# Slot stages in two phases, with half of the norm on GpSimd

## The reference

```
xn = layernorm(x)                              # 256 features
h = gelu([xn, slot_mean] @ w1.T + b1)          # 128
logits = (h @ w2.T + b2) / (|tau| + 0.1)       # 64 slots
topk_vals, topk_idx = top_k(logits, 8)
alpha = scatter(softmax(topk_vals), topk_idx)  # zero outside the 8
slot_input = einsum('bts,btd->bsd', alpha, xn) # over all tokens of a batch
gi = slot_input / (alpha.sum(tokens) + 1e-8)
S_new = GRU(gi, slots)
out = x + (alpha @ (S_new @ wv.T + bv)) @ wo.T + bo
```

## Time and profile before

| | us |
|---|---|
| median of 3 runs | 2550.9 (2548.64 to 2559.86) |
| the profiled execution: its own time | 2551.9 |
| its span, first to last instruction | 2550.1 |
| first slots stage in it | 1819.4 to 1986.2 (the next part's first instruction) |
| second slots stage in it | 2432.3 to 2550.1 |

### The profile page before, as it was taken

How to read it: one execution, slowest core, us unless ns; L and a number is a source line. 1 busy time by engine, 2 the same in 40 slices (tenths; PEclk the granted TensorE clock), 3 DMA queues, 4 the chain that set the end, 5 groups by cost and what they waited for, 6 DMA issues and landing times. The chain is left out here.

```text
span 2550.1 us, 40275 instructions
## 1 busy us (share of the span) xinstructions
PE 2180.0 (85%) x14544; PEld 1305.5 (51%) x14544; DVE 1894.2 (74%) x2586; ACT 1819.4 (71%) x3103; POOL 1615.2 (63%) x1407
## 2 busy tenths in 40 slices
PE   0798898988989989899898998987367699999967
PEld 0345454554545545455454554544234377887744
DVE  4389888898888988889888898888474455555543
ACT  0598889988899888998989989897162244444452
POOL 1089898898988989889898898989310411222010
PEclk9999999999999999999999999999668799999979
DMA  5404224043241532414314143140400211111031
GB/s 188 104 14 117 74 52 117 27 107 77 49 117 35 136 81 53 117 41 93 91 35 117 43 92 92 34 108 17 169 19 29 96 30 34 29 29 29 22 114 66
DMA packets 129930, 184.25 MB, mean 72 GB/s; under 512 B 13634, under 2 KB 76098, under 8 KB 129348
## 3 DMA queue, kind: packets, MB, share of 16 engines
q1 hardware_dynamic: 129732, 181.69, 26.6%
HBM read 134.97 MB, written 42.47 MB: 70 GB/s over the span
## 5 line engine op out<-in xcount | busy, mean ns | idle before, releaser
L617 POOL TENSOR_TENSOR h<-h,C_rep 128x512 f32<-128x512 f32 x1024 | 1274.3, 1277 | 199.4 <-ACT h_carry L536 199.4
L423 DVE TENSOR_TENSOR_SCAN h<-decay,h_carry,psum 128x512 f32<-128x512 f32 x768 | 956.1, 1271 | 126.2 <-PE psum L745 95.3
L528 ACT ACTIVATE decay<-dt_rep,A 128x512 f32<-128x512 f32 x1024 | 729.4, 713 | 101.0 <-DVE h L423 91.8
L745 PEld LDWEIGHTS psum<-ident,u_B 128*128 128x128 f32 x4096 | 476.7, 141 | 561.1 <-DVE h L423 310.2
L745 PE MATMUL psum<-ident,u_B 128*128 128x128 f32 x4096 | 630.4, 280 | 141.2 <-DVE h L423 109.0
L548 ACT ACTIVATE u_B<-u_tok,B_tok 128x512 f32<-128x512 f32 x832 | 589.2, 710 | 63.7 <-PE psum L745 45.9
L423 DVE TENSOR_TENSOR_SCAN h<-decay,zero,psum 128x512 f32<-128x512 f32 x256 | 319.0, 1271 | 54.3 <-PE psum L745 34.6
L754 PE MATMUL psum<-h,state_sum 128*32 128x512 f32 x2048 | 279.7, 619 | 11.1 <-POOL h L617 10.9
L606 POOL TENSOR_TENSOR u_B<-u_tok,B_tok 128x512 f32<-128x512 f32 x192 | 200.1, 1042 | 40.6 <-DVE u_tok L395 40.6
L1590 ACT ACTIVATE a_probs_T<-a_psum 128x512 f32<-128x512 f32 x128 | 76.4, 597 | 197.2 <-PE a_psum L1674 197.2
L1532 DVE TENSOR_REDUCE a_row_max<-a_psum 128x4 f32<-128x512 f32 x128 | 88.4, 691 | 143.3 <-PE a_psum L1665 143.3
(11 more groups left out here) (203 smaller groups left out, 2834.3 us busy)
## 6 DMA issues: line engine op xcount, KB each, us to landing
dt_rep<-dt_rows SPq DMA_DIRECT2D x256, 256.0 KB, 5.6
C_rep<-C_rows SPq DMA_DIRECT2D x256, 64.0 KB, 2.0
dt_rows<-x_dt_gated SPq DMA_DIRECT2D x16, 1024.0 KB, 4.8
x_tok<-mamba_residual SPq DMA_DIRECT2D x16, 512.0 KB
residual<-mamba_residual SPq DMA_DIRECT2D x16, 512.0 KB, 3.9
mamba_residual<-residual SPq DMA_DIRECT2D x16, 512.0 KB, 2.9
f_gru_weights<-in_slot_gru_dram SPq DMA_DIRECT2D x2, 2176.0 KB
n_x<-in_x_dram SPq DMA_DIRECT2D x4, 1024.0 KB, 10.8
```

The costliest lines, as they stand in the source:

```text
L423: dve.tensor_tensor_scan(h[:, slot(u)], dec[:, u % DEC], PS[:, u % 2], first, ALU.mult, ALU.add)\
L528: act.activation(dec[:, u % DEC], dtr[:, k % EG], ACT.Exp, scale=A[:, s // STEPS, k:k + 1]).then_inc(S["decay"], 1)
L617: pool.tensor_tensor(h[:, slot(u)], h[:, slot(u)], crep[:, k // EG], ALU.mult).then_inc(S["hc"], 1)
L745: ins = pe.transpose(PS[:, u % 2, tb * P:(tb + 1) * P], pr[:, f % 2, tb, eg], ident[:])
```

## The change

`slots` is now in two phases. In the first, all four groups go through norm, first layer, logits and top 8 (`top_k`). In the second, DVE makes the alphas of all groups (`weigh`) and PE gathers them. For this lg, top, al, et and es have a buffer for every group, and Exp, mask and division work in place in `al`; `rest` and `ex` are gone. The groups' order in the second phase is ORDER = [0, 2, 1, 3], so that a gather takes one group of each batch and its matmuls alternate between the two halves of bank 7. POOL applies the norm to tiles 4 to 7 of each group, ACT only to tiles 0 to 3. DVE runs `combine(g + 2)` before `top_k(g)`; PE runs `hidden(g)`, `features(g + 1)`, `logits(g)`. `prepare_slots` stands before both gathers.

```diff
@@ gpsimd: after the two lines of rstd @@
+                def norm_x(g):
+                    n = PER * g + PER - 1
+                    pool.wait_ge(S["nm"], n + 1)
+                    for i in range(HG_, TG):
+                        pool.tensor_scalar(xn[:, TG * g + i, 0:D], xa[:, TG * g + i], rs[:, n, i:i + 1], nm[:, n, i:i + 1],
+                                           ALU.mult, ALU.add).then_inc(S["xn_p"], 1)
-                for n in range(PER * G):
-                    rstd(n)
-                    if n == PER:
+                for g in range(G):
+                    for n in range(PER * g, PER * (g + 1)):
+                        rstd(n)
+                    norm_x(g)
+                    if g == 0:
                         pool.memset(SVo[:], 0.0).then_inc(S["zeros"], 1)
@@ vector @@
-                def routing(g):
+                def top_k(g):
...
+                def weigh(n):
+                    g = ORDER[n]
                     dve.wait_ge(S["rest"], TG * (g + 1))
-                    dve.wait_ge(S["ex"], 2 * g + 1)
-                    dve.scalar_tensor_tensor(ex[:], rest[:], NEG, ex[:], ALU.is_equal, ALU.mult).then_inc(S["mask"], 1)
+                    dve.wait_ge(S["ex"], 2 * n + 1)
+                    dve.scalar_tensor_tensor(al[:, g], lg[:, g], NEG, al[:, g], ALU.is_equal, ALU.mult).then_inc(S["mask"], 1)
...
                 for g in range(G):
-                    routing(g)
                     combine(g + 2)
+                    top_k(g)
                     if normed:
                         r_moments(g + 3)
+                for n in range(G):
+                    weigh(n)
@@ scalar @@
-                features(0)
-                hidden(0)
-                norm_x(1)
-                norm_r(2)
                 for g in range(G):
-                    features(g + 1)
+                    features(g)
+                    norm_x(g + 1)
+                    norm_r(g + 2)
+                    hidden(g)
+                for g in ORDER:
                     act.wait_ge(S["shift"], 2 * g + 1)
-                    act.activation(ex[:], ex[:], ACT.Exp).then_inc(S["ex"], 1)
+                    act.activation(al[:, g], al[:, g], ACT.Exp).then_inc(S["ex"], 1)
...
@@ tensor @@
-                        pe.wait_ge(S["xn"], 2 * g + hf + 1)
+                        if hf == 0:
+                            pe.wait_ge(S["xn"], g + 1)
+                        else:
+                            pe.wait_ge(S["xn_p"], HG_ * (g + 1))
...
+                def gather(n):
+                    for j in range(BATCH):
+                        g = ORDER[BATCH * n + j]
+                        pe.wait_ge(S["alpha"], BATCH * n + j + 1)
+                        if n:
+                            pe.wait_ge(S["aT"], j + 1)
+                        for i in range(HG_):
+                            ins = pe.transpose(PS[:, 4 + j, i * P:(i + 1) * P],
+                                               al[:, g, 2 * i:2 * i + 2].rearrange("p i s -> p (i s)"), ident[:])
+                        ins.then_inc(S["a_tp"], 1)
                     for i in range(TG):
-                        ins = pe.matmul(PS[SL * b:SL * (b + 1), 7, 0:D + 1], al[:, g % 2, i], xn[:, TG * g + i],
-                                        start=(g % GB == 0 and i == 0), stop=(g % GB == GB - 1 and i == TG - 1))
+                        for b in range(BATCH):
+                            g = ORDER[BATCH * n + b]
+                            ins = pe.matmul(PS[SL * b:SL * (b + 1), 7, 0:D + 1], al[:, g, i], xn[:, TG * g + i],
+                                            start=(n == 0 and i == 0), stop=(n == GB - 1 and i == TG - 1))
                     ins.then_inc(S["slot_mm"], 1)
...
                 for g in range(G):
+                    hidden(g)
                     features(g + 1)
-                    hidden(g + 1)
-                    logits(g + 1)
-                    if g == G - 1:
-                        prepare_slots()
-                    gather(g)
+                    logits(g)
+                prepare_slots()
+                pe.wait_ge(S["hT"], 2 * G)
+                for n in range(GB):
+                    gather(n)
```

More of the change, by code:

```diff
@@ L848, in slots @@
     PER = 2 if normed else 1
+    ORDER = [GB * b + n for n in range(GB) for b in range(BATCH)]
     xv = x.rearrange("(g i p) d -> g p i d", i=TG, p=P)
@@ L879, in slots @@
         hT = sb("hidden_feat", [P, 2, TG * P])
[L880 to L886, removed]
+        lg = sb("logits", [P, G, TG, SL])
+        top = sb("top8", [P, G, TG, TOPK])
+        al = sb("alpha", [P, G, TG, SL])
+        et = sb("top_exps", [P, G, TG, TOPK])
+        es = sb("exp_sums", [P, G, 2, TG])
         aT = sb("alpha_feat", [P, NT // 2, P])
@@ L1022, in routing @@
+                    dve.reciprocal(es[:, g, 1], es[:, g, 0]).then_inc(S["es"], 1)
+                    dve.wait_ge(S["es"], 2 * n + 2)
+                    dve.wait_ge(S["mask"], n + 1)
+                    dve.tensor_tensor(al[:, g], al[:, g],
+                                      es[:, g, 1].rearrange("p (i o) -> p i o", o=1).to_broadcast([P, TG, SL]),
                                       ALU.mult).then_inc(S["alpha"], 1)
@@ L1135, in _ @@
                 act.wait_ge(S["c1"], 1)
[L1136 to L1139 removed]
                 for g in range(G):
[L1141 removed]
+                    features(g)
[3 more added lines that the diff above has]
+                for g in ORDER:
                     act.wait_ge(S["shift"], 2 * g + 1)
[L1143 removed]
+                    act.activation(al[:, g], al[:, g], ACT.Exp).then_inc(S["ex"], 1)
                     act.wait_ge(S["shift"], 2 * g + 2)
[L1145 to L1151 removed]
+                    act.activation(et[:, g], et[:, g], ACT.Exp).then_inc(S["ex"], 1)
                 act.wait_ge(S["pre_mm"], 1)
@@ L1155, in _ @@
                 act.activation(wvo[:].rearrange("p k d -> p (k d)"), PS[:, 3], ACT.Copy).then_inc(S["wvo"], 1)
+                for n in range(G):
+                    g = ORDER[n]
+                    act.wait_ge(S["a_tp"], n + 1)
+                    act.activation(aT[:, HG_ * g:HG_ * (g + 1)].rearrange("p i t -> p (i t)"), PS[:, 4 + n % 2], ACT.Copy)\
+                        .then_inc(S["aT"], 1)
                 act.wait_ge(S["g_tp"], 1)
@@ L1260, in _ @@
                 pe.wait_ge(S["c1"], 1)
-                hidden(0)
-                logits(0)
                 for g in range(G):
+                    hidden(g)
                     features(g + 1)
-                    hidden(g + 1)
-                    logits(g + 1)
-                    if g == G - 1:
-                        prepare_slots()
-                    gather(g)
+                    logits(g)
[3 more added lines that the diff above has]
+                    gather(n)
                 pe.wait_ge(S["gi"], 1)
```

69 lines of the change are left out of this document (25 added, 44 removed).

## The result

| | before | after |
|---|---|---|
| median of 4 runs each, one chip | 2551.5 (2548.6 to 2559.9) | 2525.3 (2519.3 to 2528.9) |
| ratio, with 95% interval | | 0.989 (0.986 to 0.992) |
| profiled execution: own time, span | 2551.9, 2550.1 | 2528.9, 2527.1 |

The change gives 1.1%, 26 us by the medians; I had forecast 0.67%, 17 us. The direction was right and the size was not.

A forecast was written before the change was run, and what follows sets the result against it. It took the bound to be a program-order loop of waits through ACT, DVE, POOL and PE, 15.76 us a round. Second stage -14.8 and first -2.4 made -17.2 us, median 2534 (-0.67%), range 2524 to 2546.

The forecast's parts named there:

- Norm on POOL: Slots' norm pieces on POOL: 1.22 us each, 4 in 4.85 us, price taken from the attention stage.
- the split is no gain for the last tile: Norm shared by ACT and POOL: a group's xn complete 4.9 us after the shift, where it was 4.0.
- The path to group 3's shift: Slots stages, from start to group 3's shift: 97.9 us in the first stage, 37.2 in the second.
- From there to the last logits: Slots stages, from group 3's shift to the last logits: 15.1 us in the first, 14.2 in the second.
- my chain: Summed chain of waits from each slots stage's start to its slot sum: 132.2 us first, 70.6 second.
- The tail to the slot sum: PE after the last logits: prepare_slots 9.35 us plus two sets of transposes and paired gather, 19.15 in all, before 19.3.
- The pairing: Gather matmuls alternating between two bank halves run side by side: 32 records in 3.8 us, bounds 3.8 and 7.25.
- the rival without it: Gathers of both stages do not pair: +13.8 us, so 2547.5, no change; chance 0.08.
- a rival of 30 us over both tails: PE's clock at 1.2 GHz through both stages' tails: each some 15 us longer, +30, 2564; chance 0.05.
- the case without blocking: POOL and DVE do not block each other: 7.8 us of waits go from both stages, 2525.9; chance 0.12.
- if it gains over 6, the block is not there: Sign: a first slots stage gaining over 6 us would show that POOL and DVE do not block each other.
- The rival of dear pieces: POOL's norm pieces cost 1.5 us, not 1.22: 28 pieces add 7.8 us, 2541.5; chance 0.15.

The follow-up runs named there:

- (subtract, mult): Changed kernel with POOL's share of the slots' norm written as (x - mean) * rstd instead of x * rstd + shift: 2542.3 us, ratio 0.997.
- the same, PE kept busy: Changed kernel with POOL's slots norm as (x - mean) * rstd, plus 2 idle matmuls ahead of each half of the last group's transposes: 2532.5 us, ratio 0.993.
- the half norm alone: Kernel before with only the second half of each group's norm pieces moved to POOL, one phase and one gather after another: 2545.8 us, ratio 0.998.
- the phases alone: Changed kernel with all norm back on ACT and gathers one batch after the other, so only the two phases stay: 2539.5 us, ratio 0.996.

## Why the prediction was wrong in size

The failed step is the price of one term of the sum: "Norm on POOL: the attention stage has the same operation on POOL at the same shape, 4 in 4.85 us, 1.22 each". It was the same instruction at the same shape with other operators, (subtract, mult) in attention and (mult, add) in the change, and it measured 0.54. With it falls "the split is no gain for the last tile, the half on POOL is late by 0.8": both halves take some 2.1 us. What that price makes is seen by parts. The group's shift is the start of POOL's L941 (my sums had its end, 0.2 us later), the logits' end the start of DVE's L1005 of group 3; each pair is first and second stage, us.

| | start to group 3's shift | shift to last logits | last logits to slot sum |
|---|---|---|---|
| my forecast (1.22 us) | 97.9, 37.2 | 15.1, 14.2 | 19.2, 19.2 |
| (subtract, mult) | 98.3, 36.6 | 17.9, 17.9 | 20.2, 20.2 |
| the same, PE kept busy | 96.9, 35.1 | 13.8, 13.8 | 18.5, 18.5 |
| after (0.54 us) | 92.6, 33.0 | 13.1, 11.5 | 20.2, 20.2 |

- The path to group 3's shift was right for its price: 97.9 against 98.3, 37.2 against 36.6. With the cheap pieces it is 5.7 and 3.6 shorter (1.4 of the second is the first load of x, waited for 3.69 us in after and 5.13 with the dear pieces).
- From there to the last logits I had 15.1 and 14.2. With dear pieces it was 17.9 in both: PE waits for POOL, 12.5 us in 7 waits over both stages against 0.3 in one in after, and the clock falls; with PE kept busy it is 13.8. In after it is 13.1 and 11.5. So the price had two effects, the longer path and the clock, and I had only the first. The two errors ran against each other: 17 us of forecast gain, 9 measured at that price, 26 at the true one. That the median missed the range by only 1 us is therefore luck. With dear pieces and the clock held, the slot sums came at 129.2 and 67.5 (68.9 with the load of before): in that case my chain, 132.2 and 70.6, was 3.0 and 1.7 us too long.
- The tail to the slot sum: 20.2, not 19.2, since the first paired gather took 5.38 and 5.37 us, partly at the low clock. The pairing itself was right (3.70 for 3.8), its worth overstated: 13.8 us by the rival without it, 10.8 measured at the slot sums and 6.2 with the ends.
- The clock. "I don't expect at that place again" was right only of the place. I had priced it as a rival of 30 us over both tails, and its small form only in the range ("one dip of the clock is 2 to 4 us"). It came under the first gather, and behind the wait for the new slots in both stages, 2.7 and 2.2 us more between slot sum and end. That wait of 2.57 us stands in the kernel before too, where the fall was shorter: the slots' output took 3.66 us at the low level as here (3.78), but the 32 records behind it 13.97, not 15.81.
- Right as forecast: three table loads a stage, the mask wait gone, prepare_slots covering exponentials, top_k(3) and weighs, and POOL's rstd held up beside DVE's 2.28 us operation, at the place that I had named. The other direction, open before, shows too: DVE's multiply L974, 0.17 us elsewhere, took 0.42 at 1872.64 while a norm piece ran. The Trainium skill (SBUF — State Buffer, section "SBUF: two separate sides") has the rule for both directions: of a DVE operation with two SBUF inputs and a GpSimd operation, the one that starts first holds their shared pair of ports for the whole instruction. This trace agrees, by 3.61 us instead of 1.64 for the rstd and 0.42 instead of 0.17 for L974.
- Two agreements with the case without blocking are false. The measured median, 2525.3, is nearly its 2525.9, and my sign "if it gains over 6, the block is not there" points to it as well, for the first stage's slot sum came 8.6 us sooner. The block was there; the sign took the price of the pieces as given, and cheap pieces gain in its place.
- The rival of dear pieces (2541.5) was the wrong side to worry about: I had looked for reasons that a piece could cost more than the row, none that it could cost less. The trace of before has no POOL row with (mult, add), so the price had no measured lower bound and should have been given a far lower one: as an estimate, 0.29 us for 256 columns at DVE's rate of 2.28 us for 2048.

Open: why the attention part took 446.1 us in the one trace of before and 443.7 in after, where nothing in it differs. The kernel with the half norm alone had 443.7 as well, and so had the one with the phases alone, so neither the phases nor POOL's half is needed for it; the six other traces with attention's code as it was lie at 443.7 to 443.9. It was not followed up. The 3.9 us of the Mamba part are within what the traces of all kernels scatter there (it ends between 1817.6 and 1823.4).

## What to carry to other kernels

Take an operation's price on GpSimd only from a row with the same operators, not from one with the same shape, and write a norm there as multiply and add. Where TensorE waits ahead of dense work, as here for 2.57 us, or for 1.75 and 2.10 us in a row, price the wait with the clock that it costs behind it, and fill it with idle matmuls into a free bank if nothing else is there. Before work is split between engines, look for the round trip that bounds the stage: moving the order of the moments, with POOL's and ACT's orders behind it, was worth nearly as much here (23.7 us) as the change itself (26).

## What the hardware showed that I had not expected

- POOL's TENSOR_SCALAR of 128x256 f32 with two per-partition scalars: 0.54 us for (mult, add), 1.22 for (subtract, mult) and for (mult, subtract).
- PE's clock fell to its lower level behind a wait of 2.57 us in 20 of the 22 stage ends without idle matmuls (the eight matmuls of the slots' output took 2.9 to 3.8 us there, and 1.99 in the other two), and in the second of two waits of 1.75 and 2.10 us. It came back 9 to 10 us after the fall (after's second end, and the last group with (subtract, mult)); with idle matmuls in these waits it stayed at 0.98 to 1.00. It also fell, to 0.60 and 0.54 in two windows of 2 us, under the first gather, with PE busy without a gap for 17 us ahead.
- Behind paired gathers the same wait cost more than behind gathers one batch at a time, in most executions (ends of 33.5 to 34.8 us against 32.1 to 32.5). Why is open.
- 32 records of gather matmuls alternating between the two halves of the columns take 3.70 us, in turn 6.36 (second sets; the first sets, partly at the low clock, 5.37 and 7.89).
